# Two layers of attention and gated experts: the last gated tiles, the down products and the second attention's norm in another order

## What is computed

```
x = x + xattn0(layernorm(x), ctx)     local attention with a small feed-forward inside
x = x + ffn0(layernorm(x))            the gated feed-forward, with rounded weights and activations
x = x + xattn1(layernorm(x), ctx, ctx, mask)      16 heads of 8 features
x = x + ffn1(layernorm(x))            8 experts, one chosen per token
```

```
ffn0:   gate = silu(q(n) @ q(w_gate)), up = q(n) @ q(w_up), out = q(gate * up) @ q(w_down)
q(activation): scale = 127 / max|row|; round(row * scale) / scale
xattn1: q = layernorm(x) @ Wq, k = ctx @ Wk, softmax(q k / sqrt(8)) under the mask, @ v, @ Wo
```

## Time and profile before

| | |
|---|---|
| median of 3 runs | 244.88 us (243.72 to 244.91) |
| the profiled execution | 242.69 us |
| its span, first to last instruction | 240.9 us |
| PE busy | 189.6 us (79%), 1750 matmuls |
| DVE busy | 175.1 us (73%) |
| ACT busy | 135.0 us (56%) |
| POOL busy | 112.0 us (47%) |
| mean granted TensorE clock | 0.97 of full speed |

### The profile page before, as it was taken

The page is one execution under the profiler, slowest core; times in us unless marked ns, Lnnn a source line. Parts: engine busy times, 40 slices in busy tenths (PEclk is TensorE's granted clock), DMA queues, the critical chain, the costliest instruction groups (busy, mean ns, idle before and its releaser), DMA issues.

```text
span 240.9 us, 4754 instructions
## 1 busy us (share of the span) xinstructions
PE 189.6 (79%) x1750; PEld 136.1 (56%) x1750; DVE 175.1 (73%) x455; ACT 135.0 (56%) x271; POOL 112.0 (47%) x205
## 2 busy tenths in 40 slices
PE   0489865998584948766979988987978885899993
PEld 0368644888341748652434534534636774798883
DVE  4678889899889587869857796886566565749252
ACT  2236755929885638435767668768792347350200
POOL 8131677994497057831587885785040031000000
PEclk9999999999978579999999999999999999999999
DMA  5996040000000000000000000000000000000000
GB/s 168 345 369 257 0 155 24 0 3 0 1 3 0 0 0 3 3 3 0 3 1 4 0 3 1 0 3 0 3 1 3 0 1 3 0 3 22 24 22 22
DMA packets 4461, 8.75 MB, mean 36 GB/s; under 512 B 514, under 2 KB 3026, under 8 KB 4052
## 3 DMA queue, kind: packets, MB, share of 16 engines
q1 hardware_dynamic: 3636, 7.78, 8.8%
q10 hardware_dynamic: 800, 0.63, 0.9%
HBM read 7.89 MB, written 0.52 MB: 35 GB/s over the span
## 4 chain that ended last, share of the span: by engine, by line
PE 30%; DVE 25%; POOL 18%; issue 11%; ACT 10%; DMA 2%; SPq 1%; POOLq 0%; DVEq 0%; ACTq 0%
PE ps L1364 26%; POOL gate_pt L541 6%; PE ps L1373 5%; POOL w L431 3%; POOL rstd L410 2%; DMA wf<-weights_dram 2%; DVE stats L851 2%; DVE hid_xm L1010 2%; POOL spread L528 2%; DVE amax L1085 2%; DVE ka_mem L1051 1%; DVE mx L1202 1%; ACT gate_pt L811 1%; POOL vareps L407 1%; DVE moments L857 1%
## 5 line engine op out<-in xcount | busy, mean ns | idle before, releaser
L1202 DVE TENSOR_REDUCE mx<-ps 128x2 f32<-128x512 f32 x64 | 41.9, 686 | 13.8 <-PE ps L1364 13.5
L811 ACT ACTIVATE gate_pt<-ps 128x512 f32<-128x512 f32 x64 | 36.6, 603 | 9.7 <-PE ps L1364 9.6
L1364 PE MATMUL ps<-w,hid_xm 128*128 128x256 f16 (+1 forms) x288 | 28.7, 255 | 0.5 <-DVE hid_xm L1010 0.5
L541 POOL TENSOR_SCALAR gate_pt<-ka_mem 32x256 f16<-32x256 f16 x64 | 25.5, 398 | 4.4 <-issue 0.2
L1364 PE MATMUL ps<-gate_pt,half_c 128*128 128x512 f16 x64 | 24.2, 380 | 3.3 <-issue 1.9
L1364 PEld LDWEIGHTS ps<-w,hid_xm 128*128 128x128 f16 x288 | 24.5, 98 | 2.9 <-POOL w L423 0.7
L1364 PE MATMUL ps<-qb,gate_pt 128*128 128x256 f16 x128 | 24.7, 275 | 0.2 <-ACT gate_pt L811 0.2
L1364 PE MATMUL ps<-gate_pt,hid_xm 128*32 128x256 f32 x256 | 20.2, 390 | 0.9 <-ACT gate_pt L811 0.9
L1364 PEld LDWEIGHTS ps<-qb,gate_pt 128*128 128x128 f16 x128 | 9.8, 97 | 14.9 <-issue 8.8
L410 POOL TENSOR_TENSOR rstd<-vareps,halfs 128x2 f32<-128x2 f32 (+1 forms) x19 | 15.8, 833 | 1.6
L528 POOL TENSOR_SCALAR spread<-mx 128x16 f16<-128x16 f32 x32 | 5.9, 203 | 21.5 <-DVE mx L1202 16.1
(11 more groups left out here) (222 smaller groups left out, 510.4 us busy)
## 6 DMA issues: line engine op xcount, KB each, us to landing
stage<-weights_dram SPq DMA_DIRECT2D x2, 1024.0 KB, 11.1
wf<-weights_dram SPq DMA_DIRECT2D x4, 256.0 KB, 8.6
wf<-mask_dram SPq DMA_DIRECT2D x1, 1024.0 KB, 4.8
eb_oT<-ffw_dram SPq DMA_DIRECT2D x1, 768.0 KB, 8.0
ctx_in<-ctx_rows_dram ACTq DMA_DIRECT2D x4, 128.0 KB, 5.5
x_in<-x_dram SPq DMA_DIRECT2D x4, 128.0 KB, 3.2
gate_pt<-ctx_cols_dram SPq DMA_DIRECT2D x1, 512.0 KB, 8.5
out_dram<-ctx_in SPq DMA_DIRECT2D x4, 128.0 KB, 1.7
```

The costliest lines, as they stand in the source:

```text
L541: ins = nc.gpsimd.tensor_scalar(kz[part, n % KRING, k], ka[part, b, quad], 1.0, 0.0, ALU.mult, ALU.add)
L811: nc_act(pt[:, head % PRING].rearrange("p t n -> p (t n)"), ps[:, 2 + head % 2, :], ACT.Exp, scale=DK ** -0.5).then_inc(sig["probs"], 1)
L1202: V.tensor_reduce(mx[:, b, head:head + 2, t], score_bank(4 * n + i).rearrange("p (h n) -> p h n", h=2), AX.X, ALU.max).then_inc(sig["smax" ...
L1364: return nc.tensor.matmul(dst, lhsT, rhs, start=start, stop=stop, skip_group_check=True)
```

## The change

On PE the two gated tiles of the second pair of batches that are left (u = 6 and 7) come ahead of the turning of batches 0 and 1. On ACT tiles 4 and 5 come ahead of the rounding of batches 0 and 1, and tiles 6 and 7 ahead of the copies of their columns. The keys of batch 0 stand between the down products of batches 2 and 3, the turning of the query rows of batches 0 and 1 ahead of the other keys, and the load of the flag behind the turning of all rows. On DVE batches 0 and 1 are finished as a pair up to their normed rows before batches 2 and 3 are begun, and the flag is made between their moments and their rows. POOL makes the roots for two batches in one, and clears `kz` in two halves, each behind the rounding of a pair of batches. On ACT the high part of the last expert weights (`split_hi("m2")`, line 586) moves behind the keys. The kernel's instructions are otherwise the same; POOL has two adds and two powers fewer and one memset more.

The diff, engine by engine. ROOTS and POOL:

```diff
-         (LN_ATT, (0,)), (LN_ATT, (1,)), (LN_ATT, (2,)), (LN_ATT, (3,)),
+         (LN_ATT, (0, 1)), (LN_ATT, (2, 3)),
...
             for b in range(B):
                 pool.wait_ge(sig["ascale"], nth_scale(b, 2))
                 nc.gpsimd.tensor_scalar(g[:, b, 0], g[:, b, 0], amax[:, b, 3, 0:1], MAGIC, ALU.mult, ALU.add)\
                     .then_inc(sig["q2"], 1)
-            pool.wait_ge(sig["kscale"], 2)
-            nc.gpsimd.memset(kz[:, :, :, :], 0.0).then_inc(sig["zeros_ready"], 1)
-            for b in range(B):
-                rstd_of(LN_ATT, b)
+                if b % 2 == 1:
+                    pool.wait_ge(sig["g"], TILES * (b + 1))
+                    nc.gpsimd.memset(kz[:, b - 1:b + 1], 0.0).then_inc(sig["zeros_ready"], 1)
+            rstd_of(LN_ATT, 0, 1)
+            rstd_of(LN_ATT, 2, 3)
```

ACT (`query_columns(b)` is the pair of lines 754 and 755):

```diff
+            gate(4)
+            gate(5)
             round_gated(0)
             round_gated(1)
-            gate(4)
-            gate(5)
+            gate(6)
+            gate(7)
             gated_columns(0)
-            gate(6)
             gated_columns(1)
-            gate(7)
             round_gated(2)
             round_gated(3)
             gated_columns(2)
             gated_columns(3)
+            key_hi(0, 1)
+            act.wait_ge(sig["resmask"], 2)
+            query_columns(0)
+            query_columns(1)
+            for b in range(1, B):
+                key_hi(b, 1)
             split_hi("m2")
-            for b in range(B):
-                key_hi(b, 1)
-            act.wait_ge(sig["resmask"], 2)
-            for b in range(B):
-                act.wait_ge(sig["turned"], nth(T_QUERY, b))
-                nc_act(colsA[:, 0, b], bank(b, 0)[:, 0:T], ACT.Copy).then_inc(sig["cols_hi"], 1)
+            query_columns(2)
+            query_columns(3)
```

DVE, behind `down_scales(2)`, in place of lines 1157 to 1189:

```diff
+            ffn_residual(0)
+            ffn_residual(1)
+            att_stats(0)
+            flags()
+            att_rows(0)
+            att_rows(1)
+            ffn_residual(2)
+            ffn_residual(3)
+            att_stats(2)
+            key_lo(0, 1)
+            query_columns_lo(0)
+            query_columns_lo(1)
+            key_lo(1, 1)
+            att_rows(2)
+            att_rows(3)
+            key_lo(2, 1)
+            key_lo(3, 1)
+            query_columns_lo(2)
+            query_columns_lo(3)
```

PE (`query_turned(b)` is lines 1604 to 1607):

```diff
             gate_up(4)
             gate_up(5)
+            gate_up(6)
+            gate_up(7)
             gated_turned(0)
             gated_turned(1)
-            gate_up(6)
-            gate_up(7)
             down(0)
             down(1)
             gated_turned(2)
             gated_turned(3)
             down(2)
+            keys(0, 1)
             down(3)
-
-            for b in range(B):
+            query_turned(0)
+            query_turned(1)
+            for b in range(1, B):
                 keys(b, 1)
+            query_turned(2)
+            query_turned(3)
             pe.wait_ge(sig["flag_ready"], 3)
             general = pe.value_load(flag_i[0:1, 0:1], min_val=0, max_val=B * T * T)
-            for b in range(B):
-                pe.wait_ge(sig["rows_ready"], nth(R_ATT, b))
-                for t in range(TILES):
-                    ins = transposed(bank(b, 0)[:, t * P:(t + 1) * P], rows[:, b, t])
-                ins.then_inc(sig["turned"], 1)
```

50 lines of the change are left out of this document (26 added, 24 removed).

## The result

The changed kernel takes 243.07 us (median of 20 runs, 239.56 to 246.13); the kernel before, run beside it, 244.62 us (20 runs, 242.78 to 246.0). The ratio is 0.988, 95% interval 0.984 to 0.991: faster, by 0.9 to 1.6%. So the gain is there in both, and its size is known only to lie between 0.4 and 1.6%. The profiled execution took 240.4 us, its span is 238.6; before, 242.69 and 240.9. So 2.3 us went in the profiled pair.

What follows compares the result with a forecast made beforehand. A chain of waits between engines, none busy throughout, bounds the kernel. Last rows 2.8 us sooner, flag load 0.9 added, queries at 96.7 instead of 98.93: 2.2 sooner, 240.5 us profiled, 242.7 from the median 244.88; range 241.0 to 244.8.

Steps and rivals of the forecast that it cites:

- Gated tiles: DVE's product of tile 4 near 77.8 us, PE's tiles 6 and 7 from 78.5, first turning done at 84.1, 2.6 later.
- Second turning: PE's turning of batches 2 and 3 starts at 85.95 us instead of 87.79, gain 1.8, and takes 1.7 at full level.
- Norm of batches 0 and 1: On DVE behind 85.95 us: moments to 87.8, POOL's two-batch power to 89.05, rows ready at 90.3.
- Batches 2 and 3: DVE's norm of the second pair: rows end at 95.7 us where the last are turned at 98.49, gaining 2.8.
- The flag: Its load on PE, uncovered between the last turning and the first query product, adds 0.9 us to the path.
- What I cost at nothing: ACT's copy of last expert weights and POOL's key copies, which start sooner and end before first maxima need POOL: nothing.
- Behind the queries: From the start of the queries to the first scores, branch included: 5.58 us, left alone by the change.
- the first: Clock falls just ahead of PE's queries, adding about 1.7 us: gain only 0.5, time 244.4 us; chance 0.24.
- The second: Low clock level outlasts both batches' queries on PE, 3.8 us more: loss of 1.6, time 246.5 us; chance 0.10.
- The third: Branch depends on something unmoved, or instruction fetch takes the gain: scores start at 104.5 as now, 244.9 us; chance 0.06.
- The fourth: Full clock for first turning too, about 0.6 us let through, and median like the profile: gain 3.5, 241.4 us; chance 0.10.

Runs made afterwards that it cites:

- gated order alone: Kernel before with only the new order of the gated tiles on PE and ACT; 242.26 us, ratio 0.990 to the kernel before.
- load put back: Changed kernel with PE's flag load again behind the last keys, ahead of turning query rows 2; 240.89 us, ratio 0.989 to the kernel before.
- all but the gated order: Changed kernel with the old order of the gated tiles put back on PE and ACT; 245.40 us, ratio 1.002 to the kernel before.
- zeros in one piece: Changed kernel with POOL's zeros of the separated keys in one piece behind the last rounding, instead of two halves; 244.28 us, ratio 0.999.
- zeros behind the power: Early branch kernel with POOL's second half of zeros behind the first power, DVE's low part of keys 1 behind batches 2 and 3's rows; 243.67 us, 0.998.
- early branch: Kernel with the load put back, its branch moved right behind the load, ahead of turning query rows 2 and 3; 240.63 us, ratio 0.984.
- added products: Changed kernel with 20 more 128x512 products on PE, results unread, placed where PE waits; 241.62 us, ratio 0.987 to the kernel before.

## Why the prediction was right

The predicted 242.7 us stand against 243.07 measured; the range held it, and a gain over 0.5%, with a chance of 0.6, is what the comparison shows. Behind the scales the queries came 27.75 - 25.20 = 2.55 us sooner, where 2.2 was said. That the profiled pair shows just 2.3 is luck in part: the changed execution entered the stretch 0.62 us later, and its branch was 0.38 us shorter (3.51 instead of 3.88). Step by step, with the changed execution's 0.62 us taken off its times:

- *Gated tiles.* Right: DVE's product of tile 4 at 77.7 (said 77.8), PE's tiles 6 and 7 from 78.5, the first turning done at 83.8 (84.1).
- *Second turning.* Right: start at 85.6 (said 85.95), at the full level, in 1.94 us (1.7). It carries the gain: earlier by 2.2, shorter by 1.4.
- *Norm of batches 0 and 1.* Right in time, rows ready at 89.8 (90.3).
- *Batches 2 and 3.* The step "So this part gains 2.8" was right as a time and wrong as a credit. I put 1.8 of it to the second turning and left the rest to the split norm. The gated order alone brings the queries 3.45 us sooner; the split norm, its powers and its zeros bring nothing on top. The old order of norms would have used the earlier second turning just as well; I never worked out that case.
- *What I cost at nothing.* POOL's copies of the keys, "start sooner", were not free: they start beside the rows of batches 2 and 3 and stretch them from 1.11 to 1.61 us. I had 1.25 for these rows.
- *The flag.* Right in kind, a little high: 0.9 us said, and with the load put back the queries come 0.69 sooner. The Trainium skill's floor for such a load (DMA: Bandwidth & Descriptors, "Latency and other measured facts", about 600 ns) is above every load here, 484 to 492 ns.
- *Behind the queries.* Right: 5.58 us said, 102.21 - 96.98 = 5.23 measured. The difference is the branch, 3.88 us before and 3.51 here; it varies from 3.33 to 3.89 between profiles, which the prediction did not allow for.

Of the rivals, the first (the level falls ahead of the queries) is in neither profile of the change, but in three kernels near by (all but the gated order, zeros in one piece, zeros behind the power), at 1.3 to 1.7 us each; its chance was not idle, and whether it happened in other runs of the change is not shown. The second, both batches' queries at the low level, was not seen in any. The third did not happen; that the branch bounds the scores is shown by the early branch. The fourth asked for the full level on the first turning; where the added products gave that, it was worth 0.66 us at the queries, near the 0.6 I had let through.

## What to carry to other kernels

When several edits go together, work out the sum for each subset, above all for the one edit that moves the longest wait: here one reordering held more than the whole gain, and another edit (a register load moved from under cover to the path) gave 0.7 us of it back. A branch on a loaded flag is a piece of work of its own, 3.3 to 3.9 us here, and is placed like one: where the other engines are busy anyway. Compare executions between two of their own landmarks; the start of the stretch alone moved by 3.6 us from one profile to the next.

## What the runs showed of the hardware that I had not expected

- **POOL's work in memory slows some of DVE's.** The same four 128x128 f32 rows took 1.11 us with POOL idle, 1.61 beside its 32x256 copies, 2.37 beside a 128x2048 memset, and 1.11 again when kept apart; DVE's sums out of PSUM ran at their usual 1.1 us beside a memset. The Trainium skill (SBUF — State Buffer, "Who interferes with whom") says that operations like these can take a port pair that DVE shares with POOL, and that who comes second waits for the whole instruction. The trace agrees that it is this kind of operation that suffers, and with the wait: the first row beside the memset ended 0.09 us behind it.
- **PE starts nothing that stands behind a branch until it is over.** It took 3.3 to 3.9 us in every profile, with one packet of instructions moving inside it; begun ahead of the row turnings it held these until it was over, while work that stood ahead of it went on.
- **The granted level cannot be read off one stretch's busy time.** PE was busy 1.66 of 3.40 us in the kernel before (100.90 to 104.30) and kept 2.4 GHz; with 1.48 in all but the gated order, and 1.74 in the early branch, it got 1.2 next. The cut matters as well: the 1.39 of 94.10 to 97.50 in the change becomes 1.83 and 2.38 when the stretches are 91.67 to 95.08 and 95.08 to 98.49. What decides the level is not shown here.
